# An attention and mixture-of-experts kernel: the first head's rotation placed ahead of the later statistics on VectorE, scalar operations written with two tensors, and two waits of GpSimd taken out

## The reference

```python
xn = (x - mean(x)) / sqrt(var(x) + 1e-5)
# attention, 16 heads of 128; latent c of 128 columns
q = rope(xn @ wq);  c = xn @ w_down;  k, v = split(c @ w_up);  k = rope(k)
out = softmax(causal(q @ k.T * 128**-0.5)) @ v @ wo
# experts: sigmoid gate, best 2 of 8, and one shared expert (hidden size 176)
scores = sigmoid(xn @ gate_w.T)
top, idx = top_k(scores, 2);  top = 2.5 * top / (sum(top) + 1e-20)
routed = sum over the 2 of top * (silu(xn @ w1[e]) * (xn @ w3[e]) @ w2[e])
shared = silu(xn @ sw1) * (xn @ sw3) @ sw2
result = x + out + routed + shared
```

## Time and profile before

| | |
|---|---|
| median of 3 runs (lowest to highest) | 719.92 us (719.78 to 720.89) |
| the profiled execution: its time is its span | 719.9 us |
| TensorE matmul, busy | 695.1 us, 97% |
| TensorE weight loads | 626.4 us, 87% |
| VectorE | 631.8 us, 88% |
| ScalarE | 604.2 us, 84% |
| GpSimd | 548.6 us, 76% |
| HBM traffic | 138 GB/s over the span |

### The profile page before, as it was taken

How to read it: one execution, slowest core, us unless ns; L and a number is a source line. 1 busy time by engine, 2 the same in 40 slices (tenths; PEclk the granted TensorE clock), 3 DMA queues, 4 the chain that set the end, 5 groups by cost and what they waited for, 6 DMA issues and landing times.

```text
span 719.9 us, 15694 instructions
## 1 busy us (share of the span) xinstructions
PE 695.1 (97%) x4536; PEld 626.4 (87%) x4536; DVE 631.8 (88%) x1763; ACT 604.2 (84%) x1513; POOL 548.6 (76%) x500
## 2 busy tenths in 40 slices
PE   5799989999999999999999999999999999999997
PEld 4687878888898999999999999999999999998886
DVE  6978989999999889888988988988888898889996
ACT  4567777888788899889989889988998989889984
POOL 3466676777875779788888788878798788988881
PEclk9799999999999999999999999999999999999999
DMA  9653423443335455656457555654656554522103
GB/s 290 190 180 112 160 83 118 159 147 113 105 126 169 144 139 137 196 134 168 115 145 207 133 153 137 185 150 135 166 128 182 158 145 139 132 46 66 61 1 117
DMA packets 65571, 100.28 MB, mean 139 GB/s; under 512 B 9712, under 2 KB 38992, under 8 KB 65488
## 3 DMA queue, kind: packets, MB, share of 16 engines
q1 hardware_dynamic: 58048, 89.70, 39.9%
q0 software_dynamic: 7152, 9.34, 7.7%
q10 hardware_dynamic: 288, 0.26, 0.1%
HBM read 70.50 MB, written 28.78 MB: 138 GB/s over the span
## 4 chain that ended last, share of the span: by engine, by line
PE 82%; DVE 10%; ACT 4%; issue 3%; POOL 1%; DMA 0%; DVEq 0%; ACTq 0%; POOLq 0%
PE qk_proj L490 16%; PE scores L490 15%; PE u_acc L490 15%; PE out_acc L490 12%; PE ffn L490 9%; PE probs_t L596 8%; PE ffn L682 2%; ACT swapped L857 1%; PE ffn L656 1%; DVE rot L1357 1%; DVE rot L1364 1%; DVE acc L1413 1%; DVE scores L1373 1%; DVE pt_lo L1388 1%; DVE bn L1178 1%
## 5 line engine op out<-in xcount | busy, mean ns | idle before, releaser
L1046 POOL TENSOR_TENSOR swapped<-swapped,sin_t 128x512 f32<-128x512 f32 x128 | 167.6, 1309 | 113.1 <-DVE rot L1364 83.5
L1061 POOL TENSOR_TENSOR qk_lo<-rot,qk_hi 128x512 fp32r<-128x512 f32 x128 | 164.8, 1298 | 11.0 <-ACT qk_hi L866 7.7
L1388 DVE TENSOR_TENSOR pt_lo<-probs_t,pt_hi 128x512 fp32r<-128x512 f32 x238 | 117.6, 494 | 47.7 <-ACT pt_hi L888 47.1
L857 ACT ACTIVATE swapped<-qk_proj 64x512 f32<-64x512 f32 x256 | 151.9, 593 | 6.8 <-PE qk_proj L490 2.2
L877 ACT ACTIVATE probs<-scores,nbias 128x512 f32<-128x512 f32 (+3 forms) x256 | 134.9, 528 | 21.7 <-DVE nbias L1373 19.8
L888 ACT ACTIVATE pt_hi<-probs_t 128x512 fp32r<-128x512 f32 x238 | 104.9, 441 | 30.2 <-PE probs_t L596 19.1
L1373 DVE CUSTOM_DVE_ANT_0 scores<-scores,mask 128x512 f32<-128x512 f32 (+3 forms) x256 | 125.4, 490 | 5.4 <-PE scores L490 3.2
L1413 DVE SCALAR_TENSOR_TENSOR acc<-out_acc,rsum,acc 128x256 f32<-128x256 f32 x256 | 111.2, 476 | 6.1 <-PE out_acc L490 3.6
L596 PE MATMUL probs_t<-ident,probs 128*128 128x128 f32 x604 | 105.5, 273 | 2.8 <-DVE pt_lo L1388 2.6
L490 PE MATMUL scores<-qk_hi 128*128 128x512 f32 (+3 forms) x256 | 93.6, 365 | 1.8 <-ACT probs L877 1.5
L1357 DVE TENSOR_TENSOR rot<-qk_proj,cos_t 128x512 f32<-128x512 f32 x128 | 87.5, 684 | 8.2 <-ACT swapped L857 7.5
(11 more groups left out here) (195 smaller groups left out, 1931.7 us busy)
## 6 DMA issues: line engine op xcount, KB each, us to landing
wt<-expert_parts SPq DMA_DIRECT2D x39, 704.0 KB, 4.4
wt<-expert_parts SPq DMA_DIRECT2D x39, 512.0 KB
raw_a<-in_attn SPq DMA_DIRECT2D x8, 768.0 KB, 5.5
xs_sorted<-u_lo SPq DMA_DIRECT2D x3, 1677.0 KB, 8.2
xs<-xs_sorted SPq DMA_DIRECT2D x39, 129.0 KB, 2.5
expert_parts<-split SPq DMA_DIRECT2D x8, 352.0 KB, 2.4
expert_parts<-raw_f SPq DMA_DIRECT2D x8, 352.0 KB, 2.4
ys_tokens<-mask SPq DMA_DIRECT2D x1, 2176.0 KB, 9.4
```

The costliest lines, as they stand in the source:

```text
L857: last = ac.activation(swapped[64 * half:64 * half + 64, which, :], qk_bank[64 - 64 * half:128 - 64 * half, :], ACT.Copy)
L1046: pool.tensor_tensor(swapped[:, which, :], swapped[:, which, :], sin_t[:, :], ALU.mult).then_inc(sinm_ok[which], 1)
L1061: pool.tensor_tensor(qk_lo[:, m % 2, which, :], rot[:, which, :], f32(qk_hi[:, m % 2, which, :]), ALU.subtract).then_inc(rlo_ok[which], 1)
L1388: ve.tensor_tensor(pt_lo[:, c], turn_bank(m, j)[:, 0:n], f32(pt_hi[:, c]), ALU.subtract).then_inc(ptlo_ok, 1)
```

## The change

- VectorE: `normalised` (16 tiles), the first of the steps in `guess_std`, the one in `row_ids` and the one in `route_scores` become `scalar_tensor_tensor`, with a second tensor that changes nothing (a maximum with an operand that is never larger) or that stands for the second scalar (`rstd` broadcast along the columns). The router's score becomes twice the sigmoid, and the guard in `route_weights` 2e-20.
- VectorE: `guess_std` is cut into pieces. `rotate(0, 0)` moves from step -3 to step -4, ahead of `variance(2)`; `cos_product(0, 1)` from behind the Newton steps to between `guess_var` and `guess_first`. The wait of the last Newton step now stands in `normalised`, for batches 2 and 3.
- GpSimd: the two waits on `xn_ok` go.
- SP: the tables are loaded behind batch 1, ahead of batches 2 and 3.

```diff
-            sp.dma_start(cos_t[:, :], cos_d).then_inc(ld_table, 16)
-            sp.dma_start(sin_t[:, :], sin_d).then_inc(ld_table, 16)
-            sp.dma_start(mask[:, :], mask_d).then_inc(ld_table, 16)
+                if b == 1:
+                    sp.dma_start(cos_t[:, :], cos_d).then_inc(ld_table, 16)
+                    sp.dma_start(sin_t[:, :], sin_d).then_inc(ld_table, 16)
+                    sp.dma_start(mask[:, :], mask_d).then_inc(ld_table, 16)
...
-                if s == -LEAD:
-
-                    pool.wait_ge(xn_ok, 2 * NT)
                 sin_product(s + 3, 1)
-                if s == 1 - LEAD:
-
-                    pool.wait_ge(xn_ok, 3 * NT)
...
-            def guess_std():
-
-                t = slice(2 * NT, TT)
-                v, r, m = (rstd[:, k, t] for k in range(3))
+            late_t = slice(2 * NT, TT)
+            gv, gr, gm = (rstd[:, k, late_t] for k in range(3))
+
+            def begun(ins):
+
+                steps["route"] += 1
+                ins.then_inc(route_step, 1)
+
+            def guess_var():
                 ve.wait_ge(inv_step, B)
-                step(ve.tensor_scalar(v, mv[:, t, 1], EPS, None, ALU.add))
-                step(ve.tensor_scalar(r.bitcast(I32), v.bitcast(I32), -0.5, 1597463007.0, ALU.mult, ALU.add))
-                for n in range(3):
-                    newton(v, r, m, v if n == 2 else r)
+                begun(ve.scalar_tensor_tensor(out=gv, in0=mv[:, late_t, 1], scalar=EPS, in1=mv[:, late_t, 1], op0=ALU.add,
+                                              op1=ALU.max))
+
+            def guess_first():
+                ve.wait_ge(route_step, steps["route"])
+                begun(ve.tensor_scalar(gr.bitcast(I32), gv.bitcast(I32), -0.5, 1597463007.0, ALU.mult, ALU.add))
+
+            def guess_square():
+                ve.wait_ge(route_step, steps["route"])
+                begun(ve.tensor_tensor(gm, gr, gr, ALU.mult))
...
             def normalised(b):
+                if b >= 2:
+                    ve.wait_ge(route_step, steps["route"])
                 for t in range(NT * b, NT * b + NT):
-                    ve.tensor_scalar(xn[:, t, 0:D], acc[:, t, :], mv[:, t, 0:1],
-                                     rstd[:, 0, t:t + 1], ALU.subtract, ALU.mult).then_inc(xn_ok, 1)
+                    ve.scalar_tensor_tensor(out=xn[:, t, 0:D], in0=acc[:, t, :], scalar=mv[:, t, 0:1],
+                                            in1=rstd[:, 0, t:t + 1].to_broadcast([P, D]), op0=ALU.subtract,
+                                            op1=ALU.mult).then_inc(xn_ok, 1)
...
-                step(ve.tensor_scalar(below, mask[:, T - P:T], -1.0, None, ALU.is_ge))
+                step(ve.scalar_tensor_tensor(out=below, in0=mask[:, T - P:T], scalar=-1.0, in1=mask[:, T - P:T],
+                                             op0=ALU.is_ge, op1=ALU.max))
...
-                step(ve.tensor_scalar(score[:, :, :], score[:, :, :], 0.5, 0.5, ALU.mult, ALU.add))
+                step(ve.scalar_tensor_tensor(out=score[:, :, :], in0=score[:, :, :], scalar=1.0, in1=score[:, :, :],
+                                             op0=ALU.add, op1=ALU.max))
...
-                step(ve.tensor_scalar(tsum[:, 0, :], tsum[:, 0, :], 1e-20, None, ALU.add))
+                step(ve.tensor_scalar(tsum[:, 0, :], tsum[:, 0, :], 2e-20, None, ALU.add))
...
-                rotate(s + 3, 0)
-                cos_product(s + 3, 1)
+                if s != 1 - LEAD:
+                    rotate(s + 3, 0)
+                    cos_product(s + 3, 1)
...
                     for k in range(KD):
                         x_low(1, k, s_bank[k])
+                    rotate(0, 0)
                     variance(2)
                     latent_rows(0)
                     variance(3)
-                    guess_std()
+                    guess_var()
+                    cos_product(0, 1)
+                    guess_first()
+                    guess_square()
+                    guess_half()
+                    guess_next(gr)
...
```

More of the change, by code:

```diff
@@ L1200, in inverse_std, with guess_half, guess_next @@
                 newton(v, r, m, v)
-            def guess_std():
-                t = slice(2 * NT, TT)
-                v, r, m = (rstd[:, k, t] for k in range(3))
-                ve.wait_ge(inv_step, B)
-                step(ve.tensor_scalar(v, mv[:, t, 1], EPS, None, ALU.add))
-                step(ve.tensor_scalar(r.bitcast(I32), v.bitcast(I32), -0.5, 1597463007.0, ALU.mult, ALU.add))
-                for n in range(3):
-                    newton(v, r, m, v if n == 2 else r)
+            late_t = slice(2 * NT, TT)
[4 more added lines that the diff above has]
+            def guess_var():
+                ve.wait_ge(inv_step, B)
+                begun(ve.scalar_tensor_tensor(out=gv, in0=mv[:, late_t, 1], scalar=EPS, in1=mv[:, late_t, 1], op0=ALU.add,
[6 more added lines that the diff above has]
+                begun(ve.tensor_tensor(gm, gr, gr, ALU.mult))
+            def guess_half():
+                ve.wait_ge(route_step, steps["route"])
+                begun(ve.scalar_tensor_tensor(out=gm, in0=gm, scalar=-0.5, in1=gv, op0=ALU.mult, op1=ALU.mult))
+            def guess_next(out):
+                ve.wait_ge(route_step, steps["route"])
+                begun(ve.scalar_tensor_tensor(out=out, in0=gm, scalar=1.5, in1=gr, op0=ALU.add, op1=ALU.mult))
             def normalised(b):
+                if b >= 2:
+                    ve.wait_ge(route_step, steps["route"])
                 for t in range(NT * b, NT * b + NT):
-                    ve.tensor_scalar(xn[:, t, 0:D], acc[:, t, :], mv[:, t, 0:1],
-                                     rstd[:, 0, t:t + 1], ALU.subtract, ALU.mult).then_inc(xn_ok, 1)
+                    ve.scalar_tensor_tensor(out=xn[:, t, 0:D], in0=acc[:, t, :], scalar=mv[:, t, 0:1],
+                                            in1=rstd[:, 0, t:t + 1].to_broadcast([P, D]), op0=ALU.subtract,
+                                            op1=ALU.mult).then_inc(xn_ok, 1)
             def x_low(b, k, bank):
@@ L1544, in _ @@
                     variance(3)
-                    guess_std()
+                    guess_var()
[4 more added lines that the diff above has]
+                    guess_next(gr)
+                    guess_square()
+                    guess_half()
+                    guess_next(gr)
+                    guess_square()
+                    guess_half()
+                    guess_next(gv)
                 if b is not None and s > -LEAD:
```

## The result

| | kernel before | changed kernel |
|---|---|---|
| median (lowest to highest), 15 runs each on one chip | 721.10 us (719.59 to 721.97) | 722.52 us (721.75 to 722.82) |
| the profiled execution: span, mean granted clock | 719.9 us, 0.992 | 720.5 us, 0.995 |
| its time | about 722.0 us (below) | 722.59 us |

The ratio of the times is 1.0019, with a 95% interval of 1.0012 to 1.0026: the changed kernel is 1.4 us slower. That lies within the 0.2% which the prediction called no change, at its edge.

What follows compares the result with a forecast made beforehand. TensorE was taken to bound the kernel, inheriting VectorE's delays where it waits in the first 62 us. 0.85 (delay before batch 2's transposes) + 0.07 (router scores) = +0.9 on 719.9 gave 720.8 us, range 718.2 to 721.9.

Steps and rivals of the forecast that it cites:

- What bounds it, and who holds whom: First 62 us: TensorE waits on VectorE, whose SBUF operations wait for GpSimd's running instruction; batch 2's transposes +1.1 us.
- The small terms: Router scores in two-tensor form +0.07 us; first `xn_ok` wait removed 0; table loads before batches 2 and 3, 0.
- Rival 1: GpSimd's block before batch 2 goes through whole, holding `guess_var` to 26.6; slower, say 721.7 us; chance 0.2.
- Rival 2: Two-tensor form isn't held by GpSimd, in the Newton steps or at the scores; faster, say 718.3 us; chance 0.2.
- Rival 3: TensorE's earlier `project(1,0)` shortens the slow-clock stretch, giving 0.5 to 1.5 us back; say 719.9 us; chance 0.15.
- What TensorE makes of it: After batch 2's transposes, the 1.1 us delay costs 0.55 to 1.1, by when the clock recovers; 0.85 taken.
- The profiled execution lasted 719.9, as the median of the runs, 719.92: The base of the forecast: the profiled execution's 719.9 us taken as agreeing with the median of the runs, 719.92.
- The chances: Whole kernel: faster by over 0.2% 0.18, slower 0.26, within 0.56; the main case, 720.4 to 721.5 us, 0.45.

Runs made afterwards that it cites:

- e12: The changed kernel with GpSimd made to wait, in step 0, for the router's first pick before its subtraction into `raw_f`; 722.13 us, ratio 1.0020.
- e9: The kernel before with GpSimd made to wait, in step 0, for the router's first pick before its subtraction into `raw_f`; 720.97 us, ratio 0.9999.
- e14: The changed kernel with GpSimd's `raw_f` subtraction beside the router scores, one step ahead of them, waiting for the first pick; 722.45 us, ratio 1.0016.
- e13: The kernel before with GpSimd's `raw_f` subtraction beside the router scores, one step ahead of them, waiting for the first pick; 720.75 us, ratio 0.9999.
- e7: The changed kernel with 21 useless matmuls in TensorE's idle time before the transposes of batch 2; 721.36 us, ratio 1.0005.
- e6: The kernel before with 13 useless matmuls before `project(1,0)` and 8 before the transposes of batch 2; 719.99 us, ratio 0.9988.
- e5: e4 without the operation of `route_scores`, 1 being added to the smaller results of the pick instead; 720.17 us, ratio 0.9986.
- e8: e5 with 15 useless matmuls before the transposes of batch 2; 718.70 us, ratio 0.9970.
- e4: The changed kernel with `normalised` in the single-tensor form and GpSimd's two `xn_ok` waits put back; 720.21 us, ratio 0.9992.
- e1: The kernel before with only `normalised` changed to the two-tensor form; 721.95 us, ratio 1.0007.
- e10: e8 with GpSimd made to wait, in step 0, for the router's first pick before its subtraction into `raw_f`; 718.54 us, ratio 0.9975.
- e11: e10 with 24 matmuls of 256 columns on zeros ahead of TensorE's first transposes; 718.40 us, ratio 0.9968.
- e15: e11 with GpSimd's wait for the router's first pick moved one step earlier, ahead of the scores; 718.86 us, ratio 0.9968.

## Why the prediction was right and wrong

The forecast was too low by 1.7 us: the base by 1.2, the size of the effect by 0.5. How the delay arises was right.

**What bounds it, and who holds whom: right.** The transposes of batch 2 were forecast at 31.75 and start at 31.82. `guess_var`, `guess_first` and `guess_square` were forecast to end at 24.0, 25.3 and 26.6; they end at 24.11, 25.36 and 26.59. The group of four takes 1.67 to 1.69 (forecast 1.68). This fits the Trainium skill's rule on the ports that VectorE and GpSimd share (SBUF — State Buffer, section "SBUF: two separate sides"), with 0.81, 1.20 and 1.39 us in the changed kernel. The Trainium skill's statement that the form with two SBUF inputs that aren't bf16 halves the speed (Vector Engine (DVE) Microarchitecture Reference, section "Points that are easy to get wrong") isn't borne out: by an estimate from it the four would have taken 2.8 us, twice the 1.39, and they took 1.7.

**The small terms: right.** Router scores +0.07: the row went from 1.32 to 1.39. The first `xn_ok` wait and the table loads 0: the chain goes from the rotation into the statistics of batch 2 without a transfer in between. GpSimd's first sine product starts when `swapped` is there.

**Rival 1** (GpSimd's block goes through whole) fell: at 24.04 and at 25.28 VectorE got in between two queued GpSimd instructions. Its time, 721.7, is the nearest of the three rivals', for a reason that isn't there. **Rival 2** (the two-tensor form isn't held) fell at all three places. **Rival 3** (the clock gives it back) fell as a forecast of the time: no comparison of medians shows less than the delay. Its mechanism is there. TensorE did `project(1,0)` at the full clock, at 24.86, the clock fell 4 us later than before and the low stretch was some 3.4 us shorter. But before, the low stretch ahead of the transposes fell on `project(1,0)`, for which the chain doesn't wait, and so only 0.17 us had come back by 40 us. The recorded clocks say the same: the mean was below 0.994 in 47 of 112 executions of the kernel before, and in none of the 26 of the changed kernel and e12. Among executions of one mean clock the medians differ by 1.7 us at 0.998 (12 and 7 executions) and by 1.6 at 0.995 (31 and 11), more than the 1.4 over all. So the clock does give back some tenths over many executions, and what makes up the rest at one mean clock stays open.

**The step "What TensorE makes of it": mis-sized.** It took 0.85 us of a delay of 1.1, the middle between the half-speed work lost (0.55) and all of it (1.1). The measured cost is 1.42 in the first comparison, 1.16 (e12 over e9), 1.70 (e14 over e13) and 1.37 with the clock held up (e7 over e6), 1.4 on the mean, of which 0.07 is the scores. The lower bound's reason was a clock that returns at the same moment whatever TensorE does. In the two profiles it returned 0.7 us later, which gives back (1.1 - 0.7) / 2 = 0.2, as the 0.96 at 40 us shows. But how the low stretch falls differs from one execution to the next (below), so two profiles can't price it; and with no low stretch at all the delay is passed on in full. The term should have been at least 1.1. 1.1 + 0.07 leaves 0.2 us. In e7 over e6 a longer wait of TensorE makes 0.18 of it; between the two profiles of before and changed it isn't there, and it lies within the uncertainty of the medians. So the rest stays open. The first transposes of batch 0 start 0.11 later (7.39 after 7.28), which is already in the 1.1.

**The step "The profiled execution lasted 719.9, as the median of the runs, 719.92": wrong, and the larger error.** 719.9 is the span, from the first to the last instruction. The time of an execution is 2.1 us more, and the row "its time is its span" in the table ahead of the prediction is wrong: 722.59 with a span of 720.5 in the changed kernel, and a run of the kernel before with a span of 719.9 took 722.01. So the profile shown was of an execution of about 722.0, not of the median one. Two like numbers of different things were taken as agreement, and that hid that the base rested on three runs alone. Those happened to be low: over 15 runs the median is 721.10, and over 112 more in the four groups the group medians are 721.05 to 721.19. Of the miss of 1.7 us, 1.2 is this base and 0.5 the size of the effect. A forecast of +0.9 on 721.1 would have been 722.0.

**The chances.** Within 0.2% had 0.56 and came out, narrowly. The range had been built around a base with no uncertainty of its own; three runs that spread over 1.1 us should have given it one.

## What to carry to other kernels

Moving work ahead on one engine also fills the gaps of the engine beside it. Before, the small Newton steps ran in GpSimd's idle time, and the second `xn_ok` wait, which looked needless, was what kept `qk_lo` out of them: with both waits and the plain form the new order gains 0.9 us at the transposes and, in the median, in time; without them it loses 1.1 at the transposes and 1.4 in time. Taking a held operation away (e5) or pushing the holder back (e13) passes the hold on to the next operation with two SBUF inputs, so look for a place where nobody waits. And for an effect below 1% put the sum on a measured median of many runs and take only differences from a profile.

## What the runs showed of the hardware

**The low clock after idle time falls differently in each execution.** Of the kernel before, in the group of e5 to e8, 15 executions had a mean granted clock of 0.992 and a median of 721.56 us, and four had 0.997 and 719.82. The instructions are the same. (Three with 0.998 had 720.28: the mean doesn't order the times by itself.) So are those of e4 and e5 up to the router, and yet their stretches differ (columns as above). e4:

```profile
24.00:30.00 6.00, 1.98 (x10) 1.26 (x10) 5.42 (x19) 2.24 (x7) 2.66 (x3) 1.00 0.94 286
30.00:35.00 5.00, 5.00 (x21) 4.31 (x21) 4.13 (x9) 3.44 (x6) 2.61 (x3) 0.66 0.47 148
```

and e5:

```profile
24.00:30.00 6.00, 1.92 (x9) 1.18 (x9) 5.48 (x19) 2.18 (x7) 2.67 (x3) 0.83 0.92 289
30.00:35.00 5.00, 5.00 (x17) 4.42 (x18) 3.87 (x8) 3.50 (x6) 2.67 (x3) 0.52 0.40 136
```

The mean over the two levels is 0.66 in one and 0.52 in the other, and 21 matmuls are done instead of 17. Useless matmuls in the idle time take most of this chance away: 719.99 instead of 721.19 in e6, 718.70 instead of 720.17 in e8 over e5.

**The hold goes both ways, in one pair of rows.** GpSimd's `qk_lo` takes 1.29 us at 25.28 in the changed kernel. In e1, where it starts beside a VectorE rotation (29.72 to 30.41), it takes 1.66. GpSimd's timeline of e1:

```profile
29.88 1.66 POOL L1061 TENSOR_TENSOR qk_lo<-rot,qk_hi 128x512 fp32r<-128x512 f32 x1 [1.55 <-DVE xn L1214]
```

The best versions are e8, e10, e11 and e15, at 718.4 to 718.9 us, which these runs don't tell apart: some 0.3% under the kernel before and 0.5% under the changed one.
